# Unrolled first and last stages, token scales kept in SBUF, unread queries left out, output bias added in PSUM

## What is computed

```python
xn = _layernorm(xe, norm_w, norm_b)
xm = xn[..., :m]
qs.append(jnp.einsum('bnm,dm->bnd', xm, q_w[:, :m]) + q_b)
...
xm = attn_out[:, sl, :m]
out = jnp.einsum('bnm,om->bno', xm, o_w[:m, :m]) + o_b[:m]
...
outs.append(out + x[:, sl, :])
```

## Time and profile before

| | |
|---|---|
| median of 3 runs | 5399.69 us (5389.56 to 5416.4) |
| profiled execution | 5404.38 us, span 5402.6 us |
| PE busy | 4846.3 us, 90% |
| DVE busy | 4263.0 us, 79% |
| ACT busy | 3469.1 us, 64% |
| POOL busy | 1327.6 us, 25% |
| mean granted TensorE clock | 0.922 of full speed |
| norm stage, until its last store has landed | 0 to 89.4 us |
| first attention stage | 1399 to 4118 us |
| sliced stage | 4118 to 4373 us |
| final stage | 5256 to 5402.6 us |

### The profile page before, as it was taken

The page is one execution under the profiler, slowest core; times in us unless marked ns, Lnnn a source line. Parts: engine busy times, 40 slices in busy tenths (PEclk is TensorE's granted clock), DMA queues, the critical chain, the costliest instruction groups (busy, mean ns, idle before and its releaser), DMA issues. The chain is left out here.

```text
span 5402.6 us, 100143 instructions
## 1 busy us (share of the span) xinstructions
PE 4846.3 (90%) x34193; PEld 2161.6 (40%) x34193; DVE 4263.0 (79%) x5521; ACT 3469.1 (64%) x6164; POOL 1327.6 (25%) x875
## 2 busy tenths in 40 slices
PE   4999776689699999999999999999998879999972
PEld 2444454146233333333333333333334435555532
DVE  5999651068699999998999999999994767777726
ACT  2777310123188888888888888888886426666650
POOL 1333220036200000000000000000001219999981
PEclk9999895689699999999999999999998659999996
DMA  4110467848633343333333333343323951323206
GB/s 168 51 51 35 145 211 276 288 152 272 148 46 46 46 58 49 47 54 47 53 46 47 54 53 46 48 58 46 46 33 111 330 179 40 77 57 78 65 26 199
DMA packets 366571, 524.73 MB, mean 97 GB/s; under 512 B 67200, under 2 KB 270752, under 8 KB 349056
## 3 DMA queue, kind: packets, MB, share of 16 engines
q1 hardware_dynamic: 353280, 501.55, 38.5%
q10 hardware_dynamic: 12800, 16.78, 0.9%
HBM read 333.54 MB, written 182.32 MB: 95 GB/s over the span
## 5 line engine op out<-in xcount | busy, mean ns | idle before, releaser
L774 DVE TENSOR_REDUCE at_NM<-at_MX 128x1 f32<-128x1024 f32 (+1 forms) x3008 | 3082.1, 1050 | 343.9 <-PE at_MX L606 314.3
L716 ACT ACTIVATE at_PB<-at_S 128x512 f32<-128x512 f32 x5056 | 2720.1, 597 | 617.4 <-PE at_S L635 502.0
L606 PE MATMUL at_MX<-at_KT,at_QT 48*128 48x512 f32 (+1 forms) x5056 | 1929.0, 457 | 80.8 <-DMA at_VS<-v 57.4
L635 PE MATMUL at_S<-at_QT,at_KT 50*128 50x512 f32 (+1 forms) x5056 | 1909.8, 443 | 7.9 <-ACT at_PB L716 7.7
L647 PE MATMUL at_AV<-at_PB,at_VS 128*32 128x256 f32 (+1 forms) x18304 | 1578.3, 417 | 16.1 <-ACT at_AVS L724 13.0
L635 PEld LDWEIGHTS at_S<-at_QT,at_KT 50*128 50x128 f32 (+1 forms) x5056 | 805.8, 188 | 886.8 <-issue 480.8
L606 PEld LDWEIGHTS at_MX<-at_KT,at_QT 48*128 48x128 f32 (+1 forms) x5056 | 795.4, 191 | 333.5 <-DVE at_NM L774 221.9
L647 PEld LDWEIGHTS at_AV<-at_PB,at_VS 128*32 128x32 f32 x18304 | 365.8, 108 | 863.9 <-ACT at_PB L716 734.6
L540 POOL CAST at_NMR<-at_NMF 16x128 fp32r<-16x128 f32 x79 | 22.1, 280 | 1650.2 <-ACT at_NMF L729 1650.2
L567 POOL TENSOR_TENSOR at_SUM<-at_SUM,at_PB 128x2048 f32<-128x2048 f32 x90 | 415.8, 4620 | 10.9
L914 PE MATMUL wkv_PQ<-wkv_XT,wkv_WT 128*128 128x512 f32 x768 | 339.2, 599 | 42.3 <-DVE wkv_DL L1034 25.4
(11 more groups left out here) (204 smaller groups left out, 3782.5 us busy)
## 6 DMA issues: line engine op xcount, KB each, us to landing
moe_W<-in_w SPq DMA_DIRECT2D x64, 1024.0 KB, 10.2
at_QT<-qk SPq DMA_DIRECT2D x408, 128.0 KB, 5.5
at_KT<-qk SPq DMA_DIRECT2D x384, 128.0 KB, 7.5
qk<-r_HI SPq DMA_DIRECT2D x64, 512.0 KB, 6.7
qk<-r_LO SPq DMA_DIRECT2D x64, 512.0 KB, 6.2
at_VS<-v SPq DMA_DIRECT2D x96, 256.0 KB, 9.1
at_KT<-qk SPq DMA_DIRECT2D x96, 256.0 KB, 6.1
ycat<-wkv_Y SPq DMA_DIRECT2D x32, 512.0 KB, 2.6
```

The source lines that it names most:

```text
L606: ins = nc.tensor.matmul(MX[r][:, a, :], q_of(s)[h:h + NQ, b * P:(b + 1) * P], k_of(it, s, b * P // W)[h:h + NQ, (c + a) * W:(c + a + 1) * W],
L635: nc.tensor.matmul(SP_[item(it, s, "score", t)[1]][:, :], k_of(it, s, c)[h:h + NQ + 2, kb * P:(kb + 1) * P], q_of(s)[h:h + NQ + 2, c * W:( ...
L716: nc.scalar.activation(PB[:, t % NPB, :], SP_[r][:, :], ACT.Exp, scale=scale).then_inc(exp_done, 1)
L774: nc.vector.tensor_reduce(NM4[:, b, c:c + 1], MX[r][:, :, :].rearrange("p a n -> p (a n)"), AX_X, ALU.max, negate=True).then_inc(ring_got, 1)
```

## The change

In the norm stage the hardware loop is gone, X has four buffers, XT three, the small tiles two. VectorE's order becomes: statistics of g+1, then scaling of g. SP issues the first load ahead of the identity.

In the sliced stage the tiles XN and NB1, ScalarE's `normed`, the store to xl and the tensor xl are gone. GpSimd writes its two scales per token into `scales`, a tile [128, 16, 2, 4] that lives in SBUF for the whole program and is allocated ahead of the first stage. Query blocks and rows of slices 1 to 3 that no lane reads are not projected, not split and not stored.

The final stage is written anew as `phase_final`, unrolled. The singly normed rows are formed from x3 and the kept scale, without the mean's term, which is constant per token. VectorE adds the bias to PA in PSUM, then forms scale * X + PA for the first m columns, row by row; ScalarE forms scale * X for the others (`rest`). VectorE's result is rstd * Z + X, also row by row, and ScalarE adds -mean * rstd (XO) and issues the store. X has four buffers; AT, PA, Z, XO have two. On VectorE add and statistics of g+1 come ahead of the result of g; on ScalarE the rest of g+1 comes ahead of XO of g.

The diff, cut to its core (declarations and removed code of the old stages left out; norm stage, sliced stage, final stage):

```diff
+            for g in range(NG):
+                wait(sp, xn_done, g - NX + 1)
+                sp.dma_start(X[g % NX][:, :, :], group(x_v, g)).then_inc(x_ld[g % NX], 16)
+                if g == 0:
+                    sp.dma_start(ident[:, :], ident_d).then_inc(const_ld, 16)
...
+            def stats(g):
+                wait(dve, x_ld[g % NX], 16 * (g // NX + 1))
+                for j in range(J):
+                    ins = nc.vector.bn_stats(ST[g % 2][:, j, :], X[g % NX][:, j, :])
+                ins.then_inc(stat, 1)
+                wait(dve, stat, g + 1)
+                for j in range(J):
+                    ins = nc.vector.bn_aggr(MV[g % 2][:, j, :], ST[g % 2][:, j, :])
+                ins.then_inc(var, 1)
+
+            def normed(g):
+                wait(dve, rs, g + 1)
+                wait(dve, turned, g - 1)
+                for j in range(J):
+                    ins = nc.vector.tensor_scalar(XN[g % 2][:, j, :], X[g % NX][:, j, :], MV[g % 2][:, j, 0:1],
+                                                  RS[g % 2][:, j:j + 1], ALU.subtract, ALU.mult)
+                ins.then_inc(xn_done, 1)
+
+            stats(0)
+            for g in range(NG):
+                if g + 1 < NG:
+                    stats(g + 1)
+                normed(g)
...
+        def parts(g):
+
+            return [q for q in range(2 * CC) if q >= CC or q < len(rows(g % E4))]
+
+        def so_far(g, q):
+
+            return sum(len(parts(i)) for i in range(g)) + parts(g).index(q) + 1 if g >= 0 else 0
...
                 wait(sp, xi_done, g - NX + 1)
                 wait(sp, xs_done, g - NX + 1)
-                wait(sp, xn_done, g - NX + 1)
                 sp.dma_start(X[u][:, :, :], group(tokens(x_d), g)).then_inc(x_ld[u], 16)
...
-                wait(sp, xn_done, g + 1)
-                sp.dma_start(group(tokens(xl_d), g), XN[u][:, :, :]).then_inc(xn_st[u], 16)
...
-                    wait(sp, lo_done, 4 * g + 2 * a + 2)
+                    cs, k = (CC, P) if a else (len(rows(e)), rows(e)[0])
+                    wait(sp, lo_done, so_far(g, CC * a + cs - 1))
                     for part, tile in enumerate((HI, LO)):
                         out = qk[a, part].rearrange("(c p) t -> p c t", p=P)
-                        sp.dma_start(out[:, :, e * GT:(e + 1) * GT],
-                                     tile[u][:, 2 * a:2 * a + 2, :].bitcast(F32)).then_inc(l_st[u], 16)
+                        sp.dma_start(out[0:k, 0:cs, e * GT:(e + 1) * GT],
+                                     tile[u][0:k, CC * a:CC * a + cs, :].bitcast(F32)).then_inc(l_st[u], 16)
                 wait(sp, v_done, g + 1)
...
-                wait(pool, xn_done, g - 1)
                 wait(pool, eps1, 2 * g + 2)
-                nc.gpsimd.tensor_tensor(RS1[g % 2][:, :, :], VE1[:, :, :], nhalf[:, :, :], ALU.pow).then_inc(rs1, 1)
+                nc.gpsimd.tensor_tensor(scales[:, g, :, :], VE1[:, :, :], nhalf[:, :, :], ALU.pow).then_inc(rs1, 1)
...
-                    wait(pe, lo_done, 4 * g + 2 * a - 2)
-                    for h in range(CC):
+                    wait(pe, lo_done, so_far(g - 1, CC * a + (CC if a else len(rows((g - 1) % E4))) - 1))
+                    for h in range(CC if a else len(ks)):
...
-            def normed(g):
-                u = g % 2
-                wait(act, nb1_done, g + 1)
-                wait(act, xn_st[u], 16 * (g // 2))
-                for j in range(J):
-                    ins = nc.scalar.activation(XN[u][:, j, :], X[g % NX][:, j, :], ACT.Identity,
-                                               bias=NB1[u][:, j:j + 1], scale=RS1[u][:, 1, j:j + 1])
-                ins.then_inc(xn_done, 1)
...
-                    for c in range(CC):
+                    for c in range(CC if a else len(rows(e))):
...
-                                                  RS1[u][:, 0, j:j + 1], ALU.subtract, ALU.mult)
+                                                  scales[:, g, 0, j:j + 1], ALU.subtract, ALU.mult)
                 ins.then_inc(xi_done, 1)
-                wait(dve, xn_done, g - 1)
-                nc.vector.scalar_tensor_tensor(out=NB1[u][:, :], in0=MV1[:, :, 0], scalar=-1.0, in1=RS1[u][:, 1, :],
-                                               op0=ALU.mult, op1=ALU.mult).then_inc(nb1_done, 1)
...
-                for q in range(2 * CC):
+                for q in parts(g):
                     a, c = divmod(q, CC)
-                    wait(dve, hi_done, 4 * g + q + 1)
+                    wait(dve, hi_done, so_far(g, q))
...
+            def load_a(g):
+                b, e = divmod(g, E4)
+                ab = ao_d.rearrange("(b c h) d t -> b (h d) c t", b=B, c=CC)[b]
+                cs = chunks(e)
+                k = cs[0][1]
+                wait(sp, a_done, g - 1)
+                sp.dma_start(AT[g % 2][0:k, 0:len(cs), :],
+                             ab[0:k, 0:len(cs), e * GT:(e + 1) * GT]).then_inc(a_ld[g % 2], 16)
+
+            def load_x(g):
+                wait(sp, y_done, g - NX + 1)
+                sp.dma_start(X[g % NX][:, :, :], group(tokens(x_d), g)).then_inc(x_ld[g % NX], 16)
+
+            sp.dma_start(OW[:, :, :], ow_d.rearrange("(c p) n -> p c n", p=P)).then_inc(ow_ld, 16)
+            load_a(0)
+            sp.dma_start(OB[:, :], ob_d.partition_broadcast(P)).then_inc(ob_ld, 16)
+            load_x(0)
+            load_a(1)
+            load_x(1)
+            load_x(2)
+            for g in range(2, NGR):
+                load_a(g)
+                if g + 1 < NGR:
+                    load_x(g + 1)
...
+                wait(pool, eps, g + 1)
+                wait(pool, nb_done, g - 1)
+                nc.gpsimd.tensor_tensor(RS[g % 2][:, :], VE[g % 2][:, :], nhalf[:, :], ALU.pow).then_inc(rs, 1)
...
+                wait(pe, z_done, g - 1)
+                for j in range(J):
+                    cs = chunks(e)
+                    for c, k in cs:
+                        ins = nc.tensor.matmul(PA[u][:, j, 0:D >> e], AT[u][0:k, c, j * P:(j + 1) * P],
+                                               OW[0:k, c, 0:D >> e], start=(c == 0), stop=(c == len(cs) - 1))
+                ins.then_inc(a_done, 1)
+
...
+            def rest(g):
+                e, u = g % E4, g % 2
+                if e == 0:
+                    return
+                wait(act, x_ld[g % NX], 16 * (g // NX + 1))
+                wait(act, xo_done, g - 1)
+                for j in range(J):
+                    ins = nc.scalar.activation(Z[u][:, j, D >> e:D], X[g % NX][:, j, D >> e:D], ACT.Identity,
+                                               scale=scales[:, g, 1, j:j + 1])
+                ins.then_inc(rest_done, 1)
+
+            for g in range(NGR):
+                u = g % 2
+                if g + 1 < NGR:
+                    rest(g + 1)
+                wait(act, y_done, g + 1)
+                wait(act, nb_done, g + 1)
+                wait(act, o_st[u], 16 * (g // 2))
+                for j in range(J):
+                    ins = nc.scalar.activation(XO[u][:, j, :], Z[u][:, j, :], ACT.Identity, bias=NB[u][:, j:j + 1])
+                ins.then_inc(xo_done, 1)
+                wait(act, xo_done, g + 1)
+                act.dma_start(group(tokens(out_d), g), XO[u][:, :, :]).then_inc(o_st[u], 16)
...
+            def add(g):
+                u, mm = g % 2, D >> g % E4
+                if g == 0:
+                    dve.wait_ge(ob_ld, 16)
+                wait(dve, a_done, g + 1)
+                nc.vector.tensor_tensor(PA[u][:, :, 0:mm], PA[u][:, :, 0:mm],
+                                        OB[:, 0:mm].unsqueeze(1).to_broadcast([P, J, mm]), ALU.add).then_inc(biased, 1)
+                wait(dve, biased, g + 1)
+                wait(dve, x_ld[g % NX], 16 * (g // NX + 1))
+                wait(dve, xo_done, g - 1)
+                for j in range(J):
+                    ins = nc.vector.scalar_tensor_tensor(out=Z[u][:, j, 0:mm], in0=X[g % NX][:, j, 0:mm],
+                                                         scalar=scales[:, g, 1, j:j + 1], in1=PA[u][:, j, 0:mm],
+                                                         op0=ALU.mult, op1=ALU.add)
+                ins.then_inc(z_done, 1)
+
+            def stats(g):
+                wait(dve, z_done, g + 1)
+                wait(dve, rest_done, g - g // E4)
+                for j in range(J):
+                    ins = nc.vector.bn_stats(ST[g % 2][:, j, :], Z[g % 2][:, j, :])
+                ins.then_inc(stat, 1)
+                wait(dve, stat, g + 1)
+                for j in range(J):
+                    ins = nc.vector.bn_aggr(MV[g % 2][:, j, :], ST[g % 2][:, j, :])
+                ins.then_inc(var, 1)
+
+            def result(g):
+                u = g % 2
+                wait(dve, rs, g + 1)
+                nc.vector.scalar_tensor_tensor(out=NB[u][:, :], in0=MV[u][:, :, 0], scalar=-1.0, in1=RS[u][:, :],
+                                               op0=ALU.mult, op1=ALU.mult).then_inc(nb_done, 1)
+                wait(dve, stat, g + 1)
```

(21 more changed lines are left out.)

254 lines of the change are left out of this document (83 added, 171 removed).

## The result

The changed kernel took 5311.23 us (median of 4 runs, 5298.94 to 5322.94) against 5398.23 for the kernel before: a ratio of 0.9833, 95% interval 0.981 to 0.9856. The forecast was 5349, range 5320 to 5379. It had the direction right and somewhat over half of the size (51 us of 87): the median lies 9 us under the range. The kernel before, timed once more beside itself, gave a ratio of 0.9994 (0.998 to 1.0007); the changed one once more 5308.12 us and 0.9829 (0.9802 to 0.9857). So the miss is no matter of that one measurement.

What follows compares the result with a forecast made beforehand. Serial dependencies were taken to bound the norm and final stages, DMA the sliced one, with TensorE close behind. Terms -22, -24 and -7 sum to -53, taking 5404.4 to 5351; adjusted towards the median, 5349 us, range 5320 to 5379.

Steps and rivals of the forecast that it cites:

- hand-overs on VectorE itself: Norm stage: 0.25 us a group added to 3.1 us of VectorE work, for a period of 3.35 us.
- The walk by intervals: Sliced stage: turned copies 14.8, 8.9, 12.0 and 12.0 us apart, fifteen intervals 178.8 us against 203.8, so -25.
- I give 5 back: Sliced stage: 5 us of the gain taken off because loads would land late at times, leaving -24.
- DMA share near 0.9: Sliced stage: sign expected if the forecast held, with a share above 1 counting as wrong.
- The rule on the size of transfers: Sliced stage: shrunk query stores free next to nothing, 12.5 us of DMA a group, gain about 20 us, not 24.
- The loop: Final stage: VectorE's result, ScalarE's shifted copy, store issue, rest, statistics, result; 7.8 us a group, 7.2 for slice 0.
- The bias at no cost: Final stage: VectorE's bias add onto PSUM, 1.22 to 0.29 us by slice, hides behind the wait for ScalarE.
- Only there can time go: Whole kernel: time can go only in the norm, sliced and final stages, 491 us together; attention stages are untouched.
- The rivals: 1: Norm and sliced stages: DMA still sets them; norm -10, sliced -8, final -7, total 5379 us. Chance 0.15.
- 2 neither: Sliced stage: TensorE stays at 1.2 GHz in slices 0 and 1; sliced +26, total 5401 us. Chance 0.06.
- Rival 3: Sliced stage: TensorE's clock rises in slices 2 and 3 too, DMA then bounds; sliced -44, 5324 from the median. Chance 0.12.
- Rival 4: All stages: tiles moved by the tile of scales slow instructions; at 3% in the first attention stage, 5433 us. Chance 0.04.

Runs made afterwards that it cites:

- e4: The changed kernel with the normed rows again made by ScalarE and stored by SP, read by nobody: 5315.56 us, ratio 0.9833.
- e6: The changed kernel with slices 2 and 3 of the sliced stage projected over 128 rows, using a weight copy with zeros: 5297.87 us, ratio 0.9808.
- e7: The changed kernel without the bias add of the final stage: 5303.82 us in one execution, final stage 129.3 us.
- e2: The kernel before with only the new norm stage: 5356.7 us, ratio 0.9917.
- e9: The changed kernel with the norm stage of the kernel before: 5350.36 us, ratio 0.992.
- e1: The kernel before with only the tile of scales allocated ahead of all else, moving every tile by 512 bytes: 5400.3 us, ratio 1.0005.
- e10: The changed kernel with a small stage ahead of the first attention stage, 100 instructions that wait for nothing on every engine: 5342.69 us (one run).

## Why the prediction was wrong

The mechanisms of the three stages came in the main as argued; each term was too small, and one term was missing. The three, 24 us too small together, would have left the result in the range, at 5325; the missing one took it out.

- **Norm, -22 against -29.1.** The working gave -23.9, from a period of 3.1 us plus 0.25 "for hand-overs on VectorE itself". There are none: neighbours on VectorE overlap slightly (9.42 is 1.27 after 8.15, for an operation of 1.35), and the period is 2.99. The 15 intervals of the scaled copies shrank by 28.6 us, from 72.6 to 44.0, where the working had 23.5 with the last group's share: 5 of the 7 us. The other 2 are those taken off for transfers, which were not due; only one load behind the first came late, by 0.2 us.
- **Sliced, -24 against -31.9.** The walk by intervals gave 178.8 us for the turned copies; 178.3 were measured. The step that failed is "I give 5 back" for late landings. The tail was 15.9 us, not 17.5, and the start 0.8 shorter. That TensorE is what is late next is right; "DMA share near 0.9" is wrong by the row (0.99), and e4 shows that 0.52 MB more a group tips it.
- **The rule on the size of transfers.** The changed kernel's batch takes 48.0 us, 12.0 a group. The Trainium skill (DMA: Bandwidth & Descriptors, Rules for kernel authors) wants 128 partitions and at least 1 MiB for full bandwidth; read as in the forecast, by which the shrunk query stores "would free next to nothing", it gave 12.5 us of DMA a group. The measured period is below that, and in e6, with the same transfers, the 15 intervals average 11.1 us; so in that reading it fails here.
- **Final, -7 against -15.7.** The loop was right. The rest was priced at 1.86 from full rows; 128, 192 and 224 columns took 1.28, 1.49 and 1.60. Store issue was 0.38, not 0.48, statistics 1.8. Period 7.24 for 7.67: 6.0 us over 14. The start came out 2.7 earlier: TensorE began 4.7 us after the stage's first instruction (6.7 before), and the adds of group 1 are half as wide. -7 -6.0 -2.7 is the measured -15.7. The bias at no cost held (e7).
- **Attention, 0 against -12.5.** The step that failed is "Only there can time go", of the three edited stages, and with it "Attention windows the same within 5 us": a term put at nothing because no line of those stages is edited. The loop is 9.2 us shorter in the profiled pair, 4.4 of it in the rest, which is the pauses (6.3 to 1.8 us), and 4.9 in the clock, which differs as much between two executions of one kernel (15.5 and 29.2 in the kernel before); 4.5 more lie in front of the first unit, where repeats of one kernel differ as much (134.2 and 122.6 in the kernel before). By their medians e2 and e9 tie 10 to 13 us outside the norm stage to its edit; the pauses account for about 5, and where the others lie is not shown. e1 excludes the moved tiles. The middle stages' -4.2 is of the size by which kernels with the same code there differ (1296.4 to 1305.2).

The rivals: 1 did not come (no stage stayed with transfers as its bound), 2 neither (in batch 1, slices 0 and 1 ran at a clock of 0.79 and 0.95). Rival 3's number, 5324, was nearest, by luck: the clock stayed at 0.69, it took e6 to raise it, and transfers did not bind then either. Rival 4 fell with e1. The range was drawn from the named stages alone and had no room for one that nobody edited.

## What to carry to other kernels

Before a software pipeline is called done, follow the loop of waits from one result to the next: here two buffers sent it through ScalarE, and a third was worth more (30 us) than the whole rewrite of the stage (16 us). Where two removals lie beside each other, undo each alone: they may hold less than their sum. Allow for unedited stages with hardware loops in the range: by these runs other code ahead of one came with 5 to 10 us of pauses more or less in it, and what the clock took of it differed by 13 us between two executions of e10's kernel, and by 14 between two of the kernel before; the length of the loop in a single profile can't tell the two apart, its pauses can.

## What the runs showed of the hardware

- The turn of a hardware loop with a long body costs TensorE a pause of 2.5 to 3.7 us and then some microseconds at a lower clock: 4.5 to 9 us at each of two turns, where a boundary of straight units costs nothing. The Trainium skill (Runtime: NRT & Kernel Launch, Instruction fetch mechanics) says that a taken branch to a far target must fetch its code before it goes on; a pause at exactly the turns agrees with it, though no view shows the fetch.
- Pauses of 0.3 to 2 us inside the loop come back at the same units, most of them in two or three of the three rounds, and move to others when code ahead of the stage changes, that of other engines too: 0.4 to 2.3 us of them with the new norm stage, 6.2 to 7.1 with the old one, 9.6 to 11.9 with 100 idle waits on the four other engines ahead.
- In the sliced stage a stretch of matmuls over 64 or 32 rows ran at a granted clock of 0.5 with TensorE busy for 10.8 of 11.9 us; with the same columns over 128 rows, with zeros, the stage's later part had 0.87 (0.69 in the changed kernel), and the whole became 13 us faster (5297.87 against 5311.23).
- Adding onto PSUM took VectorE 1.23, 0.67, 0.43 and 0.29 us for 1024, 512, 256 and 128 elements, no dearer than the old add into SBUF.
